# Attention and quantised FFN on one core: the maxima's transposes moved ahead of a query correction, K's first part ahead of a step's first exponential

## The reference

```python
def reference(x, ctx, w_gate, w_up, w_down):
    q, k, v = heads(_layernorm(x)), heads(ctx), heads(ctx)      # 16 heads of 16
    scores = jnp.einsum('bhqd,bhkd->bhqk', q, k) * 0.25
    attn = jax.nn.softmax(scores, axis=-1)
    x = x + merge(jnp.einsum('bhqk,bhkd->bhqd', attn, v))
    def fp4_linear(x, w):
        return jnp.einsum('bsk,nk->bsn', fp4_quant_dequant(x), fp4_quant_dequant(w))
    n = _layernorm(x)
    h = jax.nn.silu(fp4_linear(n, w_gate)) * fp4_linear(n, w_up)
    return x + fp4_linear(h, w_down)
```

## Time and profile before

| | us |
|---|---|
| median of 3 runs | 527.06 (525.48 to 527.43) |
| the profiled execution | 523.82 |
| its span | 522.0 |
| PE busy | 486.6 |
| DVE busy | 431.3 |
| ACT busy | 373.7 |
| POOL busy | 326.5 |

### The profile page before, as it was taken

How to read it: one execution, slowest core, us unless ns; L and a number is a source line. 1 busy time by engine, 2 the same in 40 slices (tenths; PEclk the granted TensorE clock), 3 DMA queues, 4 the chain that set the end, 5 groups by cost and what they waited for, 6 DMA issues and landing times.

```text
span 522.0 us, 13665 instructions
## 1 busy us (share of the span) xinstructions
PE 486.6 (93%) x4036; PEld 383.8 (74%) x4036; DVE 431.3 (83%) x1081; ACT 373.7 (72%) x740; POOL 326.5 (63%) x471
## 2 busy tenths in 40 slices
PE   1889999999999999998858999999999999999996
PEld 0245666666665666655527899999999999999996
DVE  3778989999999999986456898889888998889764
ACT  5568989999999999977763556655665657655653
POOL 7846677667666667644444666666667666666442
PEclk9989999999999999999877999999999999999999
DMA  7764687777777667531000000000000000000000
GB/s 214 230 199 138 190 196 211 210 196 189 189 189 192 180 188 202 159 105 43 0 1 1 3 21 21 20 19 11 20 20 20 10 20 20 20 15 16 22 20 32
DMA packets 50321, 48.97 MB, mean 94 GB/s; under 512 B 4848, under 2 KB 48240, under 8 KB 50288
## 3 DMA queue, kind: packets, MB, share of 16 engines
q1 hardware_dynamic: 50288, 48.58, 33.0%
HBM read 18.94 MB, written 4.19 MB: 44 GB/s over the span
## 4 chain that ended last, share of the span: by engine, by line
PE 77%; DVE 7%; issue 5%; DMA 4%; ACT 3%; POOL 3%; SPq 1%; ACTq 0%; POOLq 0%; DVEq 0%
PE SC L1179 22%; PE PV L1179 12%; PE PV L1127 10%; PE MX L1109 10%; PE SC L1095 9%; DVE MF L802 4%; PE T L1204 4%; DMA QS<-MT 3%; PE T L1209 2%; PE T L1074 2%; PE T L1042 2%; PE SC L1204 1%; PE T L1049 1%; SPq L301 1%; PE SC L1209 1%
## 5 line engine op out<-in xcount | busy, mean ns | idle before, releaser
L802 DVE TENSOR_REDUCE MF<-MX 128x2 f32<-128x512 f32 x256 | 164.2, 683 | 20.8 <-PE MX L1109 17.1
L630 ACT ACTIVATE P<-SC 128x512 f32<-128x512 f32 x256 | 140.5, 594 | 20.2 <-PE SC L1095 18.3
L1109 PE MATMUL MX<-KS,QS 96*128 96x256 bf16 x512 | 103.7, 286 | 5.2 <-DVE MF L802 3.0
L1095 PE MATMUL SC<-QS,KS 98*128 98x256 bf16 x512 | 99.2, 276 | 2.0 <-DMA QS<-MT 1.8
L553 POOL TENSOR_TENSOR HQ<-HN,hscale 128x704 f32<-128x704 f32 x31 | 43.1, 1392 | 60.6 <-DVE HN L933 60.6
L735 ACT ACTIVATE HH<-T 128x768 fp32r<-128x768 f32 x31 | 25.2, 812 | 66.0 <-PE T L1204 66.0
L1127 PE MATMUL PV<-P,VA 128*32 128x256 f32 x1024 | 70.4, 393 | 0.9 <-ACT OT L639 0.9
L1095 PEld LDWEIGHTS SC<-QS,KS 98*128 98x128 bf16 x512 | 43.8, 98 | 34.6 <-ACT P L630 19.7
L1179 PE MATMUL SC<-WH,XH 128*128 128x352 f32 x256 | 68.5, 349 | 0.0
L1109 PEld LDWEIGHTS MX<-KS,QS 96*128 96x128 bf16 x512 | 45.1, 99 | 30.7 <-DVE MF L802 22.3
L1179 PE MATMUL SC<-WL,XH 128*128 128x352 f32 x256 | 62.9, 327 | 0.0
(11 more groups left out here) (138 smaller groups left out, 1039.5 us busy)
## 6 DMA issues: line engine op xcount, KB each, us to landing
KS<-KP SPq DMA_DIRECT2D x96, 128.0 KB, 3.3
QS<-QP SPq DMA_DIRECT2D x96, 128.0 KB, 2.4
QN<-in_x_p SPq DMA_DIRECT2D x16, 256.0 KB, 3.2
KT<-in_ctx_t SPq DMA_DIRECT2D x16, 256.0 KB, 4.5
C<-in_ctx SPq DMA_DIRECT2D x16, 256.0 KB, 3.1
X<-in_x SPq DMA_DIRECT2D x16, 256.0 KB, 4.8
out<-OB SPq DMA_DIRECT2D x32, 128.0 KB, 1.7
W<-in_L_ffn_w_up SPq DMA_DIRECT2D x5, 128.0 KB, 5.5
```

Source lines behind the costliest of these rows:

```text
L630: nc.scalar.activation(P[g % 2][:, j, :, :], SC[h % 3][:, :, :], ACT.Exp, scale=0.25).then_inc(exp_done, 1)
L802: nc.vector.tensor_reduce(MF[st.slot(off, 2)][:, :, h:h + 1], MX[h % 2][:, :, :], AX.X, ALU.max, negate=True).then_inc(mx_done, 1)
L1095: last = nc.tensor.matmul(SC[h % 3][:, k, :], KS[r][0:ROWS, h, k * 128:(k + 1) * 128], QS[r][0:ROWS, h, :], start=True, stop=True)
L1109: last = nc.tensor.matmul(MX[h % 2][:, q, :], QS[r][0:PROD, h, q * 128:(q + 1) * 128], KS[r][0:PROD, h, :], start=True, stop=True)
```

## The change

Four edits:

1. TensorE: in slot (2,3) `maxima` now stands before the query correction `queries(st, 1)`; it stood behind it. ScalarE: in slot (2,3) `maxima_out` now stands before `part_out` of part 1. In the steps below 0 `maxima_out` stays at (2,0), `maxima` at (2,2).
2. VectorE: `denominators` and `output` of the first half stand at (2,0), before the maximum of (2,1); they stood behind it.
3. ScalarE: `key_part(st, 0)` stands before the exponential of (0,0); it stood behind that of (0,2).
4. SP: four of the six DMAs for KS (the rows that take parts 0 and 1) wait for part 1 and go out first; MT follows; then the two rows of part 2, which alone wait for part 2.

```diff
+KEYS = (0, 1, 2, 0, 1, 0)
...
-                    sp.wait_ge(k_low, st.times(LEAD, 1, 1))
+                    sp.wait_ge(k_out, st.times(LEAD, 2, 2))
                     gate(sp)
                     sp.wait_ge(sc_ready, st.times(0, H, 1))
                     gate(sp)
-                    stack(KS[r], KP[st.slot(LEAD, 2)], (0, 1, 2, 0, 1, 0), r)
+                    stack(KS[r], KP[st.slot(LEAD, 2)], KEYS, r, (0, 1, 3, 4))
                 if st.has(1):
                     sp.wait_ge(mt_ready, st.times(1, 1, 1))
...
+                if st.has(LEAD):
+                    sp.wait_ge(k_low, st.times(LEAD, 1, 1))
+                    gate(sp)
+                    stack(KS[r_q(st)], KP[st.slot(LEAD, 2)], KEYS, r_q(st), (2, 5))
...
+                if st.has(LEAD):
+                    key_part(st, 0)
                 for g in range(NG):
                     for j in range(HG):
                         exp(st, g, j)
-                        if (g, j) == (0, 2) and st.has(LEAD):
-                            key_part(st, 0)
...
-                        if (g, j) == (2, 0) and st.first < 0:
+                        if (g, j) == ((2, 3) if st.first >= 0 else (2, 0)) and st.has(1):
                             maxima_out(st)
                         for n, at in enumerate(((2, 0), (2, 3), (3, 3))):
                             if (g, j) == at and st.has(LEAD):
                                 part_out(QP[st.slot(LEAD, 2)], TB, n, q_tr, q_out, st)
-                        if (g, j) == (2, 3) and st.first >= 0 and st.has(1):
-                            maxima_out(st)
...
-                        if (g, j) == (2, 1) and st.has(-1):
+                        if (g, j) == (2, 0) and st.has(-1):
                             denominators(st, 0)
                             output(st, 0)
...
-                        if (g, j) == (2, 2) and st.first < 0 and st.has(1):
+                        if (g, j) == ((2, 3) if st.first >= 0 else (2, 2)) and st.has(1):
                             maxima(st)
```

More of the change, by code:

```diff
@@ L295, in load_x, with stack @@
                              x_d[:, bass.ds(b * QT, QT), :]).then_inc(x_loaded[r], 16)
-            def stack(dst, parts, order, r):
-                for j, p in enumerate(order):
+            def stack(dst, parts, order, r, js=range(6)):
+                for j in js:
+                    p = order[j]
                     sp.dma_start(dst[j:PROD:6, :, :].rearrange("d h t -> d (h t)"),
@@ L1164, in attention_step @@
                             queries(st, 2)
-                        if (g, j) == (2, 3) and st.first >= 0 and st.has(1):
-                            maxima(st)
                         if (g, j) == (1, 3) and st.has(-1):
```

## The result

The changed kernel is faster: median 523.43 us (521.09 to 524.9, seven runs) against 527.06 us (525.48 to 527.52, seven runs), ratio 0.9939, 95% interval 0.9918 to 0.9961. On 527.06 us that is 3.2 us (2.1 to 4.3). Compared again on another occasion it came to 0.9959 (0.9935 to 0.9983). The time lies 0.03 us inside the lower bound of the stated range, and the gain is two to four times the forecast 0.9 us.

A forecast was written before the change was run, and what follows sets the result against it. TensorE bounds the kernel (93% busy), with 2.5 us lost to late maxima DMAs in eleven steps. -2.5 + 0.1 + 0.2 + 0.8 + 0 + 0.5 = -0.9 us gives 526.1 us; range 523.4 to 529.3 us.

The forecast's parts named there:

- all of the gain and none of the cost: Rival: TensorE's 0.07 us stalls vanish in its queue and step 15 has slack; -2.5 us, 524.5 us, chance 0.25.
- With MT first, MT starts at 187.25 and so does its DMA, 0.47 us sooner.: ScalarE, slot 11: copying MT before the query part starts copy and DMA at 187.25 instead of 187.72.
- inside the 2.5 us: SP's order: MT no longer held 0.87 us behind the K stack in the worst step; counted within the 2.5 us.
- The excess of 2.5 us: Eleven full attention steps: 156.73 us less eleven undisturbed steps of 14.02 us, lost to late maxima DMAs into QS.
- Second correction, +0.8 us: TensorE, slot 11: query part ends at 188.11, wanted at 188.09; stall about 0.07 us in each of eleven steps.
- Maxima's transposes, +0.2: TensorE, slot 11: transposes moved earlier may stall for MP; 0.02 us a step, 0.2 us in all.
- Step 15, +0.5: VectorE: WDL subtraction now behind reciprocal and product, delaying TensorE's weights transpose; bounds 0 and 0.70 us, once.
- K's part first, 0: ScalarE, step's start: 0.64 us of K's part 0 moves into the wait for the first score; cost and gain 0.
- The slower rival, ScalarE as the bound: Step's start: KP not ready in the gap, every exponential slips 0.64 us a step; +4.5 us, 531.6 us, chance 0.12.
- What stays late, 0.1 us: MT's transfer: the longest, 3.34 us, might still be late; between 0 and 0.3 us left, 0.1 taken.
- A transfer that still takes 3 us and arrives late: Sign of a wrong prediction: MT's DMA in the changed kernel still taking 3 us and arriving late.

The follow-up runs named there:

- the floor of 153.97 us: Kernel before with scores of 96 of 98 rows that don't wait for MT's transfer: eleven steps 153.97 us, ratio 0.9934 to the kernel before.
- 153.92 us: Changed kernel with scores of 96 rows that don't wait for MT's transfer: eleven steps 153.92 us, ratio 0.9925 to the kernel before.

## Why the prediction was right or wrong

The measured time lies in the range, and the wait that I named is the one that the gain comes from: without it the kernel before is at 0.9934. The size was wrong (0.9 us forecast; 3.2 us, then 2.2 us measured), and one step named the wrong edit. By the prediction's own bound for what can be told from no change (524.4 us) the result is faster, to which it gave 0.22 against 0.64 for no change. The rival nearest to what came is the first, all of the gain and none of the cost (524.5 us, chance 0.25).

1. *"With MT first, MT starts at 187.25 and so does its DMA, 0.47 us sooner."* This step failed. In the kernel before, the transfer can hardly start sooner, because SP is in the K stack: maxima first alone gives 1.0017, SP issues MT 0.80 us behind the copy's start, and the issue comes 0.13 us sooner, not 0.47. It could be read in the trace of before (below): SP's last K row there runs to 187.29 + 0.61 = 187.90, 0.28 us before MT's issue, so 0.47 us were not free. I had written of SP's order that it matters in the worst step and lies "inside the 2.5 us"; it is the edit on which the gain hangs (0.9959 alone, 1.0033 for the change without it). That the time fell inside the range owes something to luck: the change makes both edits, and the margin is 0.03 us.
```profile
187.29 0.61 SPq L301 DMA_DIRECT2D KS<-KP  x1
...
188.18 0.66 SPq L376 DMA_DIRECT2D QS<-MT  x1
188.19 0.38 PE L1049 MATMUL T<-QP,negidentb 128*128 128x512 bf16 x1
```

2. *The excess of 2.5 us.* Against the floor of 153.97 us the profiled execution had 2.8 us and the second one 2.2, so as a reading of traces it was right. Timed, the wait is worth 3.5 us (1.7 to 5.2), which takes in both. The profiled 523.82 us were below all seven timed runs of that occasion, but on the later ones the same kernel ran from 522.1 us up, with medians of 525.6 to 526.0; so it is not shown that this execution was an unusual one.
3. *Second correction, +0.8 us: not there.* The query part is ready at 187.16 + 0.60 = 187.76, the weight load goes at 187.81, and the matmul at 187.84 is 1.44 us behind the exponential's start at 186.40, exactly as 188.09 belonged to a matmul at 188.19, 1.44 us behind 186.75. The load slipped by 0.07 us as worked out; the matmul did not, since the load stood 0.10 us ahead of its matmul before and 0.03 us is enough. The deadline came from the matmul's start and not from the load that I had read. The kernel with maxima first alone has the same 1.44 us (187.16 to 188.60).
4. *Maxima's transposes, +0.2: not there.* The load does wait for MP at 186.52 (0.21 us idle), but the next score's place is unmoved: undisturbed steps are 13.99 to 14.07 us against 14.02.
5. *Step 15, +0.5: there, 0.32 us.*
6. *K's part first, 0: held.* It starts behind the last QP and the first exponential comes 0.57 us behind the first score's start instead of 0.50 (190.47 to 191.04; before 176.78 to 177.28). I had expected 0.17 us of delay; the next score covers it. The slower rival, ScalarE as the bound, did not come.

```profile
190.04 0.65 ACT L601 ACTIVATE QP<-T 128x512 bf16<-128x512 f32 x1
190.47 0.39 PE L1099 MATMUL SC<-QS,KS 98*128 98x256 bf16 x2
190.52 0.68 ACT L610 ACTIVATE KP<-KT 128x512 bf16<-128x512 f32 x1
...
191.04 1.14 ACT L636 ACTIVATE P<-SC 128x512 f32<-128x512 f32 x2
```

7. *What stays late, 0.1 us: too small.* The change's two executions are 2.1 and 0.7 us over 153.92 us. With the stack out of the way I expected about 2.0 us for a transfer, or at most 3.34 if nothing got shorter; they reach 4.45 us. A transfer that still takes 3 us and arrives late was named as a sign of being wrong, and it came. The shortening that I had drawn from the Trainium skill (DMA: Bandwidth & Descriptors, Queues, rings and completion order) is not seen in the late ones. The 2.0 us that the prediction took from the Trainium skill (the same page, Anatomy of one DMA) are a fit for DMAs issued from GpSimd, and this one leaves SP; the shortest that any chain here shows took 2.27 us. How long the transfers took that came in time no row shows, as nobody waited for them.

With the costs that were not there taken out, the traces give -2.8 + 0.3 and what stays late: -1.1 us with the 1.4 us that the change's two executions still lose on average, -2.5 us if no transfer were late. Over all profiles it is about the same: the eleven steps took 156.45 us on average in the two of the kernel before and 155.22 in the seven with SP's order, 1.2 us less, of which step 15 takes 0.3 back. The comparisons' 2.2 and 3.2 us are 1.1 to 2.3 us more than these sums give, and the traces do not explain the rest. A pair of them could not: what follows the eleven steps took 306.1 and 307.4 us in two executions of the kernel before, 306.2 and 307.4 in two of the change.

## What to carry to other kernels

Before pricing an earlier producer, look at what its consumer's queue is doing at the new time: here a copy moved 0.47 us forward was worth nothing until the six issues in front of its DMA (3.8 us of SP's time) were split around it. For such a wait, measure its whole worth by a kernel that doesn't have it, and take the deadline of an operand from the start of its matmul, not from where the weight load before it happens to stand. A rare late transfer makes a single profile a poor base for a difference under 1%.

## What the runs showed of the hardware

- The same 16 KB transfer, where it is on a chain and so late, took 2.27 to 3.75 us with the old SP order, 2.71 to 4.45 us with the new one and 4.34 to 4.99 us from ScalarE's queue. With SP's order and the wait in place, seven profiles (of six kernels) had 13 late transfers in 77 steps, five of them in the first full step. What sets the long ones stays open; they came without the K stack directly ahead and from either queue.
- Issuing that DMA held SP's queue 0.66 us, and ScalarE 0.64 us, 0.87 with its wait for its own copy.
- VectorE's small cast of the maxima takes 0.17 us or 0.38 to 0.41, by where it falls beside GpSimd's instruction on the weights. In the kernel before:

```profile
114.39 0.94 POOL L502 TENSOR_SCALAR WC<-WC 128x288 f32<-128x288 f32 x1
114.88 0.17 DVE L823 CAST MP<-MF 128x32 bf16<-128x32 f32 x1
...
142.89 0.94 POOL L502 TENSOR_SCALAR WC<-WC 128x288 f32<-128x288 f32 x1
143.47 0.39 DVE L823 CAST MP<-MF 128x32 bf16<-128x32 f32 x1
```

Started 0.49 us behind GpSimd's start it runs through; started 0.58 us behind, it ends at 143.86, 0.03 us after GpSimd's end. In the eleven steps two casts are short (started up to 0.51 us behind) and nine long (0.56 us or more). The Trainium skill, SBUF — State Buffer, Who interferes with whom, has a cast in a 2-port mode and a GpSimd instruction exclude each other for a whole instruction, by the order of issue; the long cast agrees, the short one, which runs inside GpSimd's instruction, does not, as far as the profile's rough spans on GpSimd can tell.
